# Half of an adjacency update moved to ScalarE and GpSimd, shorter routing, and another order in the first batch and the tail

## The reference

```python
def xattn(h, adj_raw, Wq, Wk, gamma_raw):          # h: 4 x 512 x 128, adj_raw = layernorm(x)
    sim = einsum(Q, K) / (sqrt(d) * H)              # 512 x 512 per batch, heads summed
    threshold = top_k(sim, 153)[-1]                 # per row
    A = sigmoid(sim) * (sim >= threshold)
    A = (A + A.T) * 0.5
    gamma = sigmoid(gamma_raw)
    return (1 - gamma) * adj_raw + gamma * A

x = x + xattn(ctx, layernorm(x), Wq, Wk, gamma_raw)
x = x + moe(layernorm(x))
# moe: scores = sigmoid(x @ router_w); groups of 4 experts, the best 4 of 8 groups are masked OUT,
# then the best 8 of the 32 experts; routed expert FFNs (silu(x Wg) * (x Wu)) Wd with weights,
# plus one shared FFN of width 512 for every row
```

## Time and profile before

| | us |
|---|---|
| median of 3 runs | 1066.85 (1064.3 to 1068.14) |
| profiled execution, its own time | 1066.63 |
| span of its trace | 1064.8 |
| TensorE matmul busy | 918.4 (86%) |
| VectorE busy | 577.8 (54%) |
| ScalarE busy | 487.4 (46%) |
| GpSimd busy | 437.2 (41%) |
| mean granted TensorE clock | 0.934 |

### The profile page before, as it was taken

The page is one execution under the profiler, slowest core; times in us unless marked ns, Lnnn a source line. Parts: engine busy times, 40 slices in busy tenths (PEclk is TensorE's granted clock), DMA queues, the critical chain, the costliest instruction groups (busy, mean ns, idle before and its releaser), DMA issues.

```text
span 1064.8 us, 21255 instructions
## 1 busy us (share of the span) xinstructions
PE 918.4 (86%) x4604; PEld 495.4 (47%) x4605; DVE 577.8 (54%) x1320; ACT 487.4 (46%) x993; POOL 437.2 (41%) x348
## 2 busy tenths in 40 slices
PE   3258698879787999999999999999999999999994
PEld 1143354545343555554545545555544554545542
DVE  5958898889764443446343454444455454453321
ACT  5276563742132443446444454444455454463331
POOL 2011101110032455555655554645545565655643
PEclk8569888798888999999999999999999999999998
DMA  5211120111338578777887778687887787876654
GB/s 170 75 41 52 40 87 7 40 43 40 102 107 268 117 165 178 164 170 206 186 199 145 176 164 218 125 205 176 179 207 173 220 181 210 184 168 122 122 103 72
DMA packets 90267, 149.25 MB, mean 140 GB/s; under 512 B 9648, under 2 KB 46768, under 8 KB 90224
## 3 DMA queue, kind: packets, MB, share of 16 engines
q0 software_dynamic: 33120, 80.64, 38.6%
q1 hardware_dynamic: 57104, 68.13, 19.5%
HBM read 101.55 MB, written 47.20 MB: 140 GB/s over the span
## 4 chain that ended last, share of the span: by engine, by line
PE 47%; issue 9%; DVE 5%; ACT 4%; DVEq 3%; ACTq 3%; DMA 1%; SPq 0%; POOL 0%; POOLq 0%
PE bank L258 40%; PE bank L1484 4%; PE bank L1475 3%; ACT gu L240 3%; DVEq L1170 2%; ACTq L1170 2%; DVE gu L247 1%; DMA stage_dn<-in_L_ffn_w_down_dram 1%; DVE hid L1400 1%; DVE dn L250 1%; DVE hT L1409 1%; ACT silu L1263 0%; PE bank L1456 0%; ACTq L240 0%; DVE mark_p L400 0%
## 5 line engine op out<-in xcount | busy, mean ns | idle before, releaser
L258 PE MATMUL bank<-gu,xgT 128*128 x1764 | 408.6, 382 | 11.9 <-issue 7.6
L1213 POOL DMA_INDIRECT out_dram<-y,ids_i x145 | 242.2, 1671 | 283.4 <-DMA out_dram<-y,ids_i 156.9
L258 PEld LDWEIGHTS bank<-gu,xgT 128*128 128x128 f16 x1764 | 173.1, 98 | 193.7 <-issue 22.9
L258 PE MATMUL bank<-dn,hT 128*128 x870 | 212.1, 380 | 15.9 <-issue 15.8
L1201 POOL DMA_INDIRECT xg<-xrows,ids_i x153 | 158.8, 1038 | 64.2 <-issue 41.4
L1400 DVE SCALAR_TENSOR_TENSOR hid<-bank,xg,silu 128x256 f32<-128x256 f32 x146 | 70.3, 482 | 207.3 <-ACT silu L1263 207.3
L1275 ACT CAST hT<-bank 128x256 f16<-128x256 f32 x146 | 53.7, 368 | 224.9 <-PE bank L1475 224.9
L1282 ACT ACTIVATE y<-bank 128x512 f32<-128x512 f32 x145 | 86.6, 597 | 133.5 <-PE bank L258 133.5
L1409 DVE TENSOR_TENSOR hT<-bank,hT 128x256 f16<-128x256 f32 x146 | 61.7, 423 | 150.7 <-ACT hT L1275 150.7
L258 PEld LDWEIGHTS bank<-dn,hT 128*128 128x128 f16 x870 | 85.0, 98 | 90.6 <-issue 23.3
L247 DVE SCALAR_TENSOR_TENSOR gu<-stage_gu,gu (+1 forms) x64 | 75.6, 1222 | 48.1 <-ACT gu L240 48.1
(11 more groups left out here) (217 smaller groups left out, 770.2 us busy)
## 6 DMA issues: line engine op xcount, KB each, us to landing
stage_gu<-in_L_ffn_w_gate_dram SPq DMA_DIRECT2D x32, 512.0 KB
stage_gu<-in_L_ffn_w_up_dram SPq DMA_DIRECT2D x32, 512.0 KB
stage_dn<-in_L_ffn_w_down_dram SPq DMA_DIRECT2D x32, 512.0 KB
x_sb<-in_x_dram SPq DMA_DIRECT2D x4, 1024.0 KB, 6.9
xrows<-adj SPq DMA_DIRECT2D x4, 1024.0 KB, 4.2
out_dram<-acc SPq DMA_DIRECT2D x4, 1024.0 KB, 4.7
xg<-xrows,ids_i POOLq DMA_INDIRECT x153, 4.4
out_dram<-y,ids_i POOLq DMA_INDIRECT x145, 5.1
```

Of the source, the lines that this page charges most:

```text
L258: last = nc.tensor.matmul(out_ap, stationary(a, c), moving(w, c), start=(c == 0 and (a, w) == parts[0]), stop=(c == chunks - 1 and (a, w) ...
L1213: g_.indirect_dma_start(out, bass.IndirectOffsetOnAxis(ap=ids_i[:, t:t + 1], axis=0), y[:, t % YS, :], None, compute_op=ALU.add).then_inc( ...
```

## The change

Six things change together.

1. In the update, `adj` times gamma/2 is written to `under` by ScalarE (`scaled_adjacency`, semaphore `adj_scaled`), placed ahead of `s_high(p, 3)`; GpSimd adds it to `acc` (semaphore `half_ready`), placed behind the four `s_low` in its queue; VectorE adds the transposed bank times gamma/2 to `acc` in one operation, which waits for both `adjT_ready` and `half_ready`. The separate scale-and-add goes.
2. Routing: the pairwise maxima and minima of four tiles become one operation each, and so does the masking by groups.
3. In the first batch the copies of constants come first, `inverse_stds`, the gains and coefficients go behind the counts of `bound(0)`, and ScalarE's sigmoids behind its counts.
4. The conversions of the shared weights in batch 0 are later: the low part of the first half after `search_step(1, 0)` and `coefficients(1)`, high and low part of the second half at the end of the batch. The statistics of the next x are all in `update` for batch 0.
5. In the last batch TensorE does `rank_tokens` and `count_columns` ahead of `s_gate_up(3, 1)`, and VectorE does `s_add(2, 3)` behind `s_product(3, 0)`.
6. In the tail `tab` and `onehot` are f16, and ScalarE copies the table ahead of the last `s_high`.

```diff
-        tab = early("tab", [P, B, 2, P])
+        tab = early("tab", [P, B, 2, P], F16)
...
@@ gpsimd, per batch, behind the base and s_low(b - 1, 0..3)
+                    for i in range(RT):
+                        a = acc[:, b * RT + i, :]
+                        pool.wait_ge(S["adj_scaled"], RT * b + i + 1)
+                        pool.wait_ge(S["base_ready"], RT * b + i + 1)
+                        nc.gpsimd.tensor_tensor(a, under[:, i, :], a, ALU.add).then_inc(S["half_ready"], 1)
@@ tensor, last batch
                         sum_marks(pe, p)
-                        s_gate_up(pe, b, 1, (0,))
                         rank_tokens(pe, b)
                         count_columns()
-                        s_gate_up(pe, b, 1, (1,))
+                        s_gate_up(pe, b, 1)
@@ scalar
+                def scaled_adjacency(b):
+                    for i in range(RT):
+                        act.wait_ge(S["adj_ready"], RT * b + i + 1)
+                        nc.scalar.activation(under[:, i, :], adj[:, i, :], ACT.Identity, scale=gcol[:, 3:4]).then_inc(S["adj_scaled"], 1)
...
                 root(1, slice(1, 3))
+                for k in range(STEPS):
+                    counts(0, k, range(DVE_TILES, RT))
                 act.wait_ge(S["small_loaded"], 3 * 16)
                 nc.scalar.activation(gcol[:, 1:2], gcol[:, 0:1], ACT.Sigmoid).then_inc(S["gamma_ready"], 1)
                 sigmoids(0)
-                for k in range(STEPS):
-                    counts(0, k, range(DVE_TILES, RT))
...
                         mixed(b + 1)
+                    scaled_adjacency(b)
                     if p >= 0:
                         s_high(act, p, 3)
...
                         sigmoids(b + 1)
-                        if p < 0:
-                            convert_high(act, 1)
                         counts(b + 1, 3, range(RT))
                         s_silu(act, b, 0)
                         counts(b + 1, 4, range(RT))
                         s_silu(act, b, 1)
+                        if p < 0:
+                            convert_high(act, 1)
@@ vector
+                def gains():
+                    inverse_stds(1, slice(1, 2))
+                    dve.wait_ge(S["gamma_ready"], 1)
+                    ch.done(v.tensor_scalar(gcol[:, 2:3], gcol[:, 1:2], -1.0, 1.0, ALU.mult, ALU.add))
+                    ch.step(v.tensor_scalar(gcol[:, 3:4], gcol[:, 1:2], 0.5, None, ALU.mult))
+                    coefficients(0)
...                                                  in bound(b), behind the four counts
+                    if b == 0:
+                        gains()
...
-                    if b + 1 < B:
+                    if 1 <= b < B - 1:
                         x_stats(b + 1, range(0, RT // 2))
...                                                  in update(b, nth)
-                    dve.wait_ge(S["adj_ready"], RT * b + RT)
-                    dve.wait_ge(S["base_ready"], RT * b + RT)
...
-                        x_stats(b + 1, range(RT // 2, RT))
-                    for i in range(RT):
+                        x_stats(b + 1, range(RT // 2 if b else 0, RT))
+                    for i in range(RT):
+                        a = acc[:, b * RT + i, :]
                         dve.wait_ge(S["adjT_ready"], RT * b + i + 1)
-                        v.tensor_tensor(tmp[:, i, :], adj[:, i, :], bank[SIMB[i % 2]][:, :], ALU.add).then_inc(S["adjT_used"], 1)
+                        dve.wait_ge(S["half_ready"], RT * b + i + 1)
+                        v.scalar_tensor_tensor(a, bank[SIMB[i % 2]][:, :], gcol[:, 3:4], a, ALU.mult, ALU.add).then_inc(S["adjT_used"], 1)
                     dve.wait_ge(S["adjT_used"], RT * b + RT)
-                    for i in range(RT):
-                        a = acc[:, b * RT + i, :]
-                        ch.done(v.scalar_tensor_tensor(a, tmp[:, i, :], gcol[:, 3:4], a, ALU.mult, ALU.add))
...                                                  in routing(b)
-                    for c in range(RT):
-                        ch.done(v.tensor_tensor(pmx[:, c, :, :], q[:, c, :, :, 0], q[:, c, :, :, 1], ALU.max))
-                        ch.done(v.tensor_tensor(pmn[:, c, :, :], q[:, c, :, :, 0], q[:, c, :, :, 1], ALU.min))
+                    ch.done(v.tensor_tensor(pmx[...], q[:, :, :, 0], q[:, :, :, 1], ALU.max))
+                    ch.step(v.tensor_tensor(pmn[...], q[:, :, :, 0], q[:, :, :, 1], ALU.min))
...                                                  the masking by groups likewise, one operation for four
...                                                  in the order by batch
                     bound(b)
-                    if b == 0:
-                        convert_low(dve, 0)
                     nth = update(b, nth)
...
                         find_keys(dve, ch, p)
+                    else:
+                        convert_low(dve, 0)
                     low_rows(b)
...
                         search_step(b + 1, 4)
+                        if p < 0:
+                            convert_low(dve, 1)
                     else:
                         s_product(dve, b, 0)
+                        s_add(dve, p, 3)
                         find_keys(dve, ch, b)
...
-        onehot = sb("onehot", [P, 2 * B, NT])
+        onehot = sb("onehot", [P, 2 * B, NT], F16)
...                                                  scalar, second block
                 s_silu(act, b, 3)
+                copy_table(act, b)
                 s_high(act, b, 3)
-                copy_table(act, b)
```

More of the change, by code:

```diff
@@ L155, in xattn_moe_kernel @@
             "ident_zero consts pool_consts const_step qk_loaded small_loaded ctx_loaded x_loaded zeroed "
-            "mix_ready mix_copied ctxT_ready hT_ready u_ready u_copied sim_ready sim_copied gamma_ready "
+            "mix_ready mix_copied ctxT_ready hT_ready u_ready u_copied sim_ready sim_copied gamma_ready adj_scaled half_ready "
             "squares_ready dve_step var_ready sqrt_ready coef_ready base_ready "
@@ L432, in xattn_moe_kernel @@
         adj = sb("adj", [P, RT, N])
-        under = tmp = sb("under", [P, RT, N])
+        under = sb("under", [P, RT, N])
         xT32 = under[:, :, :].rearrange("p i (k t) -> p i k t", k=KC)
@@ L970, in update @@
                     if more:
-                        x_stats(b + 1, range(RT // 2, RT))
-                    for i in range(RT):
-                        dve.wait_ge(S["adjT_ready"], RT * b + i + 1)
-                        v.tensor_tensor(tmp[:, i, :], adj[:, i, :], bank[SIMB[i % 2]][:, :], ALU.add).then_inc(S["adjT_used"], 1)
-                    dve.wait_ge(S["adjT_used"], RT * b + RT)
+                        x_stats(b + 1, range(RT // 2 if b else 0, RT))
                     for i in range(RT):
                         a = acc[:, b * RT + i, :]
-                        ch.done(v.scalar_tensor_tensor(a, tmp[:, i, :], gcol[:, 3:4], a, ALU.mult, ALU.add))
-                    ch.settle()
+                        dve.wait_ge(S["adjT_ready"], RT * b + i + 1)
+                        dve.wait_ge(S["half_ready"], RT * b + i + 1)
+                        v.scalar_tensor_tensor(a, bank[SIMB[i % 2]][:, :], gcol[:, 3:4], a, ALU.mult, ALU.add).then_inc(S["adjT_used"], 1)
+                    dve.wait_ge(S["adjT_used"], RT * b + RT)
                     for i in range(RT):
@@ L1018, in routing @@
                     ch.step(v.tensor_tensor(sg[:, :, :], scores[:, :, :], bias[:, :].unsqueeze(1).to_broadcast([P, RT, E]), ALU.add))
-                    q = sg[:, :, :].rearrange("p i (g a c) -> p i g a c", a=2, c=2)
-                    for c in range(RT):
-                        ch.done(v.tensor_tensor(pmx[:, c, :, :], q[:, c, :, :, 0], q[:, c, :, :, 1], ALU.max))
-                        ch.done(v.tensor_tensor(pmn[:, c, :, :], q[:, c, :, :, 0], q[:, c, :, :, 1], ALU.min))
-                    ch.settle()
+                    q = sg[:, :, :].rearrange("p i (g a c) -> p (i g) a c", a=2, c=2)
+                    ch.done(v.tensor_tensor(pmx[:, :, :, :].rearrange("p i g a -> p (i g) a"), q[:, :, :, 0], q[:, :, :, 1], ALU.max))
+                    ch.step(v.tensor_tensor(pmn[:, :, :, :].rearrange("p i g a -> p (i g) a"), q[:, :, :, 0], q[:, :, :, 1], ALU.min))
                     ch.done(v.tensor_tensor(t1[:, :, :], pmx[:, :, :, 0], pmx[:, :, :, 1], ALU.max))
@@ L1038, in routing @@
                         search_step(b + 1, 2)
-                    for i in range(RT):
-                        ch.done(v.tensor_tensor(masked[:, i, :].rearrange("p (g c) -> p g c", c=EG), sg[:, i, :].rearrange("p (g c) -> p g c", c=EG),
-                                                gkeep[:, i, :].unsqueeze(2).to_broadcast([P, GROUPS, EG]), ALU.mult))
-                    ch.settle()
+                    ch.step(v.tensor_tensor(masked[:, :, :].rearrange("p i (g c) -> p (i g) c", c=EG), sg[:, :, :].rearrange("p i (g c) -> p (i g) c", c=EG),
```

(21 more changed lines are left out.)

## The result

The change makes the kernel slower: 1075.97 us against 1067.08 us for the kernel before on the same chip, ratio 1.0083 with a 95% interval of 1.0057 to 1.0110. In a later comparison on another chip it took 1073.30 against 1068.04, ratio 1.0048 (1.0030 to 1.0067). Forecast was 1068.5, with a range up to 1072.5. The sign of the sum was right, its size was not.

A forecast was written before the change was run, and what follows sets the result against it. VectorE bounds the attention batches, TensorE the unchanged loop from 400 us; only the part before about 326 us counts. Terms +3.3, +4.0, +0.5, -1.8, -2.9, -1.4 = +1.7, giving 1068.5 us; own range 1065.5 to 1070, wider 1061.5 to 1072.5.

The forecast's parts named there:

- The end of the first block: Last batch: ranks and columns come first, so the engines join 7.4 us after the routing, not 10.3: -2.9 us.
- Its own lower end: End of the first block with TensorE's clock down: the join gains only -1.4 us.
- The update: Batches 1 and 2: bank reads wait for GpSimd's adds behind its last residual, similarities start later: +2.0 us each.
- Batch 3: Update without following similarities: the adds end later and the statistics start at about 10.7 against 10.2, +0.5 us.
- Batch 0: First batch's new order: late low parts of shared weights and TensorE's low clock delay batch 1's masking by +3.3 us.
- Routing: Merged small operations and masks save 0.6 us in each of batches 1 to 3: -1.8 us.
- Tail: After the first block: down projection starts 3.6 us sooner but loses 2.2 to the low clock: -1.4 us.
- the lower end named: Tail: gain of up to -3.6 us if TensorE's clock stays up for the down projection.
- Rival C: Batch 0: GpSimd's base blocks VectorE's two-input operations one for one through the shared port, 1072.0 us; chance 0.29.
- A: Update: GpSimd's queue doesn't matter, batches 1 and 2 cost 0, batch 3 saves 2.7; 1061.3 us; chance 0.08.
- B: Batch 0 keeps its lead, TensorE starts by 92 and stays warm, or the down projection does: 1062.3 us; chance 0.20.
- the extra microsecond a batch: Update: if reads with one PSUM input also lost beside GpSimd's adds, up to 1 us a batch more, 1071.5 in all.

The follow-up runs named there:

- The filled kernels: TensorE idle stretches filled with matmuls nobody reads; ratios to before: kernel after, all three stretches 0.9980, only the block's end 1.0001; kernel before with new end order 0.9981.
- the second profile: The kernel after, unchanged, measured and profiled once more on another chip: 1073.30 us, masking of batch 1 at 109.92.

## Why the prediction was wrong, by its steps

**The end of the first block, -2.9: the step that failed.** It assumed "idle before about 1.8 us, because batch 3 delays TensorE by 2". Measured idle time is 4.53 us, the clock was 0.50, and the stretch came out at +1.3 (34.31 - 33.63, and 0.6 of shorter routing to be added): 4.2 us off, about half of the miss in the first profile and more than all of it in the second, where the spans are 5.4 apart and the forecast 1.7. Its own lower end, -1.4 "with it down", was wrong too. That figure compared with the kernel before, whose low stretch lay under 12 matmuls ahead of the ranks (4.00 us for ten of them); in the new order the ranks, columns and all 24 lie in it. The filled kernels reach -2.8 with the clock up, so the join's time was reckoned rightly. But most of that is not the order: it set a new order at the full clock against an old one at the low clock, and like for like the new order is worth 0.65 us at the full clock (30.85 against 31.50) and loses 1.3 to 1.5 at the low one.

**The update, +2.0 a batch.** The mechanism stands in every row: residual first, then adds, first read 6.56 us after the masking (forecast 6.4), pitch 1.23 (taken 1.16), squares awaited 5.00 us (forecast 4 or more). The size was low. Between the maskings it came to 2.64 and 1.55 net of routing's -0.6, so 3.2 and 2.2: +5.4 instead of +4.0. Part is the chain's step that I took as fixed: the similarities began 2.44 later and then took 5.36 us, 0.94 more, with a clock of 0.72 in that stretch where it had been 0.88. This share scatters: the group took 4.57 to 5.36 us over the seven profiles with this update and GpSimd's queue as here, and by masking 1 to 2 of the same profiles batch 1 costs 2.5 to 3.2 us. The windows:

```profile
121.40:126.80 5.40, 5.39 (x11) 1.98 (x10) 3.50 (x9) 2.06 (x6) 0.00 (x0) 0.72 0.01 3
```

```profile
114.90:119.40 4.50, 4.43 (x11) 1.72 (x10) 4.43 (x8) 2.06 (x6) 0.00 (x0) 0.88 0.00 0
```

The first is the kernel after, the second the kernel before. Batch 3: +0.8 for +0.5.

**Batch 0, +3.3.** Measured +4.0 in the first profile, +2.9 in the second. Single terms erred and balanced. "Under" took 2.91, not 4.5; it was GpSimd's base that stretched, to 4.99. The masking lost 1.0 and not 0.6. The three low pieces took 3.5 us beside the base of batch 1, not 5.5, so the low rows ended 1.8 us sooner, at 72.6 against 74.3, where the forecast had them unmoved. Sigmoid's wait (1.65) and the last piece (94.5 for 95.1) came as forecast; that the sum of these terms fits is in part luck. The clock cost 3.0 us, not 2.0: 8.30 against 5.34. In two kernels with the same batch 0 it cost 1.3 and 1.4, so the 2.0 lay inside the scatter.

**Routing, -1.8.** It held at -0.6 a batch.

**Tail, -1.4.** Measured -0.7. Lists 0.75, idle 3.56 as forecast; the 48 matmuls lost 2.8 us to the clock and not 2.2; over the profiles with 3.56 or 3.57 us of idle time they lost 1.4 to 2.8. With the stretch filled it is -3.6, the lower end named.

**The rest.** 1.4 us of the first profile's difference lies in the loop, and the second profile has it with the other sign. Sum of the steps as measured: 4.0 + 5.4 + 0.8 - 1.8 + 1.3 - 0.7 + 1.4 = 10.4, the spans' difference. In the second profile, with the same order of terms: 2.9 + 5.3 + 0.8 - 1.8 + 1.3 - 0.7 - 2.3 = 5.5, with the spans 5.4 apart.

**Rival C** priced a loss by the port in batch 0 at 1072.0. A total of this kind came, but not by it: "under" stayed far below the 5.5 us at which it was to decide. A and B were wrong. Of B's condition, TensorE starting by 92 and staying at the full clock, filling made the second part true (the group began at 92.95 and took 5.35), and it paid.

The Trainium skill, GPSIMD Engine Reference, section Specifications, names VectorE's instructions with two SBUF inputs as those that contend with GpSimd. The trace agrees on the pairs, and shows that either side can pay. Where VectorE's low parts and low rows (two SBUF inputs) lay beside GpSimd's base, the first two low parts took 2.36 us as alone and GpSimd 8.14 for 3.03. Where GpSimd's first add lay beside the fourth masking, VectorE paid, 1.75 us for 0.75. The new reads with one PSUM input took 0.75 instead of 0.69 beside the adds, so the extra microsecond a batch that I priced apart did not come.

What stays open: why the low stretch fell on the down projection with the update undone and with the update alone, and why the totals of the first of these and of the kernel with routing, end and tail alone scatter over 7 us, was not separated from chance.

## What to carry to other kernels

Before work is taken out from in front of a TensorE group that others wait for, look at what TensorE then does: an idle stretch of 3.6 to 5.8 us here cost 1.3 to 4 us more behind it, left 0.7 of the tail's gain of 3.6 us, and made the new order of the block's end a loss. Either leave real work in the gap, or fill it. And before a gain is put down to an order, see that both sides of the comparison had the same clock: of 2.8 us measured here 0.65 were the order's. When work is handed to another engine's queue, ask what stands at the queue's head and when that can end; here the same four adds cost 6 us more behind an instruction with a late input than in front of it.

## What was not expected of the hardware

- After 0.93, 0.69, 0.27 and 2.07 us without a matmul the next 24 took 5.34 or 5.35 us; after 4.35, 4.53, 5.45 and 5.78 us they took 8.24, 8.17, 7.90 and 8.30 (before the ranks, with some small matmuls between, in all of these but 2.07, 0.69 and 5.78). But after 5.69 and 5.72 us, in the kernels with the old end and with the update undone, they took 6.65 and 6.73. From 4.3 us up the loss was 1.3 to 3.0 us, and the idle time did not tell which.
- The same code, twice profiled, had the masking of batch 1 at 111.06 and 109.92 us, so one profile fixes such a stage only to about 1 us. The group in front of it began 0.98 us apart; its low stretch accounts for 0.16.
- GpSimd's two-input add of 128x512 f32 took 1.23 us in a row (VectorE's like operation 0.69). Its one-input base went from 0.76 to 2.0 us each beside VectorE's low parts and low rows; the longest, 3.96 us, outlasted the low parts (3.5 us in a row, not slowed).
- One of GpSimd's two-input adds beside the masking of four tiles stretched it from 2.74 to 3.75 us, all in the one operation that it met; ScalarE's passes alone beside it left it at 2.74.
